# Two semaphore waits among GpSimd's indirect DMAs: every second scatter, and the third and fifth gather of a unit

## The chip, the cores and the metric

The kernel runs on one core of a Trainium2 chip. The metric is device time in microseconds (us) of one execution, taken without a profiler, as the median of several runs. Five engines work side by side on the core, each with its own stream of instructions in program order: PE (TensorE, matrix products), DVE (VectorE), ACT (ScalarE), POOL (GpSimd) and SP (SyncE, which here only issues DMAs). They meet through semaphores: an instruction or a DMA adds to a counter, and `wait_ge` holds an engine until a counter has reached a value. An engine that waits holds back all that stands behind in its stream. A DMA adds 16 to its semaphore in all, when all of it has landed.

## The reference, cut to what matters

There are 12,500 nodes with 64 features and 400,000 edges (`src`, `dst`, 16 attributes each), sorted by `dst`. A first graph network of three layers is followed by a second one that also uses the attributes, and each ends in a residual sum and a layer norm.

```
# first network, three times
agg = segment_sum((x * out_norm)[src], dst, 12500) * in_norm
x   = elu(agg @ W + b)
x   = layernorm(x0 + x)
# second network
ea  = edge_attr @ W_edge.T + b_edge
msg = relu(x[src] + ea)
h   = x + segment_sum(msg, dst, 12500)
h   = batchnorm(h @ W1.T + b1); h = relu(h); h = h @ W2.T + b2
out = layernorm(x + h)
```

What matters for the change is `x[src]` of the second network: for each edge, the row of the source node is needed.

## The kernel before, in words

**Counting (about the first 2,000 us of the profile).** A matrix of counts is built, how many edges lead from each node to each other node, window by window of 512 destination nodes, and stored in HBM (`counts`). With it the three layers of the first network become dense matrix products. POOL issues indirect DMAs here too (L997, L1006), which the change doesn't touch.

**Dense stage.** For 3 layers times 25 windows SP loads the counts back in pieces of 896 KB, seven to a window (L789, `load_piece`), and PE multiplies them (L2182). A piece is only loaded over an old one when PE has used that (semaphores `s_pused`). Beside it the edges of the first five windows of nodes are sorted by source block: 1,430 tiles of 128 edge records of 72 bytes, ten tiles to a "granule", 143 granules. SP loads a granule (`take_records`, L796) into one of two buffers, and before that waits until the granule two back has wholly been scattered (`s_put`). PE and DVE rank the records (L1428 to L1450). POOL then waits for the load (`s_take`) and for the ranks of five tiles (`s_rowi`), and writes each tile with one indirect DMA to its rows of `sorted_recs` in HBM (L1051, `put_records`): 1,430 scatters. SP's stream is in order and written out: piece loads and record loads stand in one row, a record load after about every 3.75 piece loads.

**Edge stage.** It begins when the scatters and the dense stage are done. There are 345 units of five tiles of unsorted edges. For each tile POOL gathers 128 rows of 256 bytes from `table32` in HBM into SBUF (L1086, `gather_units`): 1,725 gathers. Their buffers are a ring of six units; before a unit POOL waits until DVE has used the unit six back (`s_gmsg`). DVE adds the gathered rows to the edge terms (`add_rows`, L1652), ACT and PE follow. Beside the units the sorted records are handled in 294 "chunks", nearly one for every unit: DVE L1645, L1673, L1680, PE L2304 to L2344. DVE's order within a step with a chunk is: prepare the next chunk, chunk hots (L1673), source hot (L1645), `add_rows` (L1652), chunk low (L1680), unit hots (L1660), unit low (L1665).

**Tail.** About 100 us: the end of the batch norm, the last product, the layer norm and the stores.

On POOL nothing but the change's own two places is edited. All of the work after the counting stage that POOL does is the two lines L1051 and L1086, and both issue indirect DMAs whose descriptors POOL itself writes. The semaphores that the change waits on exist already: `s_put` (two, by the granule's parity) is waited for by SP (L795, L886) and DVE, `s_grow` (six, by the unit's place in the ring) by DVE (L1648).

Of the kernel before, what the change touches and what calls it, by code (L numbers as in the profile page):

```python
# [28 lines left out]
UNIT = 5  # L29
GRAN = 2 * UNIT  # L30
# [274 lines left out]
STEP_OF = [n * GATHERS // len(CHUNKS_S) for n in range(len(CHUNKS_S))]  # L305
CHUNK_IN = {step: j for j, step in enumerate(STEP_OF)}
UNIT_NODES = 224


def node_range(g):  # L310
# [7 lines left out]
def plan_bases():  # L318
# [4 lines left out]
    while sum(r[1] for r in runs) < len(ranges):  # L323
        at = sum(r[1] for r in runs)
        best = None
        for base in range(max(SORTED * WIN, ranges[at][1] - UNIT_NODES), ranges[at][0] + 1):
            for step in range(2 * GRAN * P // 16):
                n = 0
                while at + n < len(ranges) and ranges[at + n][1] - UNIT_NODES <= base + n * step <= ranges[at + n][0]:
                    n += 1  # L330
# [8 lines left out]
UNIT_BASE = [BASES[n // 2] for n in range(GATHERS)]  # L339
UNIT_WINDOWS = [sorted({b // WIN, (b + UNIT_NODES - 1) // WIN}) for b in UNIT_BASE]  # L340
BEGINS = {w: min(n for n in range(GATHERS) if w in UNIT_WINDOWS[n]) for w in range(SORTED, WINDOWS)}
# [6 lines left out]
ROW_RING, REC_RING, ATTR_RING, HOT_RING = 6, 4, 4, 4  # L348


def gnn_kernel(nc, x, src, dst, dst_rows, edge_runs, edge_recs, attr, w_l0, b_l0, w_edge, b_edge, w1, b1, gamma, beta,
               w2, b2, out):
    ctx = ExitStack()
    with ctx:
# [148 lines left out]
        def keys_of(a, b):  # L503
            return keys_a[:, a:b] if b <= KEYS_A else keys_b[:, a - KEYS_A:b - KEYS_A]
# [38 lines left out]
        c_hot = tmp16[:, 0:2 * CHUNK_TILES * WIN].rearrange("p (s k n) -> p s k n", s=2, k=CHUNK_TILES)  # L543
        g_hot = onehot_h[:, 0:HOT_RING * UNIT * UNIT_NODES].rearrange("p (s k n) -> p s k n", s=HOT_RING, k=UNIT)
        g_base = tmp_row[:, CHUNK_TILES * WIN:CHUNK_TILES * WIN + len(BASES)]
# [142 lines left out]
        s_put, PUT0 = s_near[2:4], [16 * (b - a) for a, b in SETS[2:4]]  # L688
# [7 lines left out]
        s_grow = [*gathered_sems.rows[0], *gathered_sems.rows[1], *gathered_sems.rows[2]]  # L696
# [245 lines left out]
        def _(pool):  # L942
# [100 lines left out]
            def put_records():  # L1043

                for g in range(RANKED // GRAN):
                    pool.wait_ge(s_take[g % 2], TAKE0[g % 2] + 16 * (g // 2 + 1))
                    for n in range(2):
                        pool.wait_ge(s_rowi, ROWI0 + g * 2 + n + 1)
                        for k in range(UNIT):
                            t = (g * 2 + n) * UNIT + k  # L1050
                            G.indirect_dma_start(out=sorted_recs[:, :], out_offset=bass.IndirectOffsetOnAxis(ap=keys_of(t, t + 1).bitcast(I32), axis=0),  # L1051
                                                 in_=taken[g % 2][:, n * UNIT + k, :], in_offset=None).then_inc(s_put[g % 2], 16)

            rank_tables()
            put_records()
            pool.wait_ge(s_bounds, 1)
            pool.wait_ge(s_bounds, 1)
# [21 lines left out]
            def gather_units():  # L1079

                for n in range(GATHERS):
                    if n >= ROW_RING:
                        pool.wait_ge(s_gmsg, n - ROW_RING + 1)
                    for k in range(UNIT):
                        t = (FIRST_UNIT + n) * UNIT + k
                        G.indirect_dma_start(out=g_rows[:, n % ROW_RING, k, :], out_offset=None, in_=table32[:, :],  # L1086
                                             in_offset=bass.IndirectOffsetOnAxis(ap=src_key[:, t:t + 1], axis=0)).then_inc(s_grow[n % ROW_RING], 16)

# [8 lines left out]
            with pool.Else():  # L1097
                pool.wait_ge(s_dtable, 16 * WINDOWS)
                bases(g_base).then_inc(s_bases, 1)
                gather_units()  # L1100

        @block.vector
        def _(dve):
# [4 lines left out]
            def link(ins):  # L1108

                chain[1] += 1  # L1110
                ins.then_inc(chain[0], 1)
                dve.wait_ge(chain[0], chain[1])
# [121 lines left out]
            def edge_bounds():  # L1234
# [14 lines left out]
                over, under = (g_ext[0:1, 2 + n, 0:len(BASES)] for n in range(2))  # L1249
                link(V.scalar_tensor_tensor(out=over, in0=greatest, scalar=-float(UNIT_NODES), in1=base_check, op0=ALU.add, op1=ALU.is_ge))  # L1250
                link(V.scalar_tensor_tensor(out=under, in0=least, scalar=float(SORTED * WIN), in1=base_check, op0=ALU.max, op1=ALU.is_lt))
# [373 lines left out]
            def sorted_edge_sums():  # L1625
# [29 lines left out]
                def unit_hots(n):  # L1655
                    if n >= HOT_RING:
                        dve.wait_ge(s_gused, n - HOT_RING + 1)
                    for k in range(UNIT):
                        t = (FIRST_UNIT + n) * UNIT + k
                        last = V.tensor_scalar(g_hot[:, n % HOT_RING, k, :], iota_win[:, 0:UNIT_NODES], dst_key[:, t:t + 1], None, ALU.is_equal)  # L1660
                    last.then_inc(s_ghot, 1)
# [791 lines left out]
```

## Time and profile before

| | us |
|---|---|
| median of 3 runs | 5930.82 (5928.49 to 5935.44) |
| span of the profiled execution | 7586.7 |
| POOL busy | 3774.9 (50% of the span) |
| PE busy | 5556.9 (73%) |
| DVE busy | 4274.3 (56%) |
| ACT busy | 2271.1 (30%) |

The profiled execution's own time is given by its span alone; it is 1,656 us, or 28%, longer than the median of the unprofiled runs. So the profile says how long instructions and landings take and in which order things happen, but it has gaps that the unprofiled runs can't all have. "Busy" for POOL is the time in which it writes the descriptors of an indirect DMA; the transfer itself comes later and is seen only as packets of the DMA queue q0 (software_dynamic). Queue q1 holds what SP issues. In the rows, "remote" and "another core or an unknown queue" are waits whose releaser the profile can't name, on a single core, and "issue" is time in which the engine waited for nothing that is shown.

### The profile page before, as it was taken

Reading aid. Unit: us, or ns where it says so; the run is one execution under the profiler, and the core shown is the slowest. Engines: PE = TensorE matmul, PEld = TensorE weight load, DVE = VectorE, ACT = ScalarE, POOL = GpSimd, SP = SyncE. Lnnn points to the kernel's source line nnn. Section 1 sums busy time; section 2 is a strip of 40 time slices with the busy share of each in tenths; the row PEclk is TensorE's granted clock in tenths of the full one; section 3 lists DMA queues with packets and bytes.
Section 4 is the critical chain, followed back from the end, with each engine's and each line's share of the span. In section 5 each row is a group of like instructions: output and inputs, shape, how many; then the busy total and the mean of one; then the engine's idle time right before and its main releaser. Section 6 shows DMA issues by size and latency. Waiting matters only on the chain.

```text
span 7586.7 us, 112214 instructions
## 1 busy us (share of the span) xinstructions
PE 5556.9 (73%) x39907; PEld 3224.8 (43%) x39908; DVE 4274.3 (56%) x14548; ACT 2271.1 (30%) x4057; POOL 3774.9 (50%) x3824
## 2 busy tenths in 40 slices
PE   6599799997777777778777774666766666665666
PEld 5366566665433333333433332333433333333334
DVE  5488888899533333333444112666666665555556
ACT  2487688873100000000001111333333322222223
POOL 4323233354354544545554556565655666665663
PEclk9799899999888988888888886888888888878887
DMA  2333333331555655556556661111111111111111
GB/s 99 140 130 119 120 142 137 118 118 64 177 173 188 197 177 180 186 186 195 184 185 193 218 207 41 32 34 33 33 33 33 34 33 32 33 33 32 32 32 34
DMA packets 438341, 828.25 MB, mean 109 GB/s; under 512 B 161611, under 2 KB 266983, under 8 KB 430951
## 3 DMA queue, kind: packets, MB, share of 16 engines
q1 hardware_dynamic: 305430, 713.88, 27.9%
q0 software_dynamic: 117952, 81.54, 5.1%
q10 hardware_dynamic: 14400, 25.61, 1.2%
q8 instruction: 323, 5.29, 0.3%
q14 instruction: 236, 1.93, 0.1%
HBM read 621.34 MB, written 199.35 MB: 108 GB/s over the span
## 4 chain that ended last, share of the span: by engine, by line
PE 24%; another core or an unknown queue 14%; issue 13%; DVE 11%; PEld 2%; ACT 1%; PEldq 0%; DVEq 0%; ACTq 0%
PE banks L2182 10%; PE banks L2344 4%; DVE tmp L1673 4%; PE banks L2271 2%; PE banks L2304 2%; PEld banks L2182 2%; DVE onehot L1660 2%; DVE rows_f L1652 2%; PE banks L2324 2%; PE banks L2331 1%; PE banks L2164 1%; DVE rows_f L1680 1%; DVE rows_f L1665 1%; PE banks L2157 1%
## 5 line engine op out<-in xcount | busy, mean ns | idle before, releaser
L1086 POOL DMA_INDIRECT rows_f<-table,src_key x1725 | 1708.4, 990 | 1103.4 <-DVE rows_f L1652 604.3
L1051 POOL DMA_INDIRECT sorted_recs<-onehot,rows x1280 | 1235.5, 965 | 1260.6 <-DMA onehot<-edge_recs_dram 718.7
L2182 PE MATMUL banks<-wide,rows_f 128*128 128x512 fp8e4 (+1 forms) x4900 | 1268.1, 400 | 355.4 <-issue 352.3
L1867 ACT ACTIVATE wide<-banks 128x784 fp8e4<-128x784 f32 x1563 | 1205.6, 825 | 484.6 <-PE banks L2104 340.6
L1006 POOL DMA_INDIRECT onehot<-edge_runs_dram,rows_f x472 | 596.2, 1263 | 1149.1 <-DVE onehot L1196 935.9
L2104 PE MATMUL banks<-rows_f 128*128 128x196 f16 (+2 forms) x7525 | 1004.1, 258 | 223.6 <-ACT wide L1867 138.7
L2104 PEld LDWEIGHTS banks<-rows_f 128*128 128x128 f16 x7525 | 708.5, 152 | 612.1 <-ACT wide L1867 401.9
L2271 PE MATMUL banks<-w_edge_blk,rows 80*128 80x320 f32 x690 | 337.4, 578 | 762.9 <-DVE rows_f L1652 521.6
L1444 DVE SCALAR_TENSOR_TENSOR onehot<-banks,onehot 128x98 f16<-128x98 f32 (+2 forms) x1113 | 295.6, 266 | 989.9 <-PE banks L2164 504.1
L1342 DVE TENSOR_TENSOR rows_f<-hid 128x1024 f16<-128x1024 f16 (+1 forms) x1016 | 679.4, 669 | 300.8 <-PE banks L2104 169.5
L1645 DVE TENSOR_SCALAR rows_f<-banks,iota_p 128x512 f16<-128x512 f32 x294 | 220.7, 751 | 1067.0 <-remote 638.8
L2182 PEld LDWEIGHTS banks<-wide,rows_f 128*128 128x128 f16 x4900 | 454.9, 103 | 817.2 <-issue 510.3
L2069 PE MATMUL banks<-wide,onehot 128*128 128x392 fp8e4 x3125 | 791.5, 334 | 9.2 <-issue 8.9
L2182 PE MATMUL banks<-wide,hid 128*128 128x512 fp8e4 (+1 forms) x2450 | 650.1, 401 | 126.3 <-issue 125.2
L1347 DVE TENSOR_TENSOR rows_f<-rows_f,tmp 128x1568 f16<-128x1568 f16 (+1 forms) x874 | 714.4, 817 | 0.0
L2344 PE MATMUL banks<-tmp,rows_f 128*128 128x512 f16 x2058 | 676.6, 485 | 0.0
L1673 DVE TENSOR_SCALAR tmp<-iota_win,rows 128x512 f16<-128x512 f16 x2058 | 638.0, 379 | 0.0
L1899 ACT ACTIVATE rows_f<-banks 128x512 f16<-128x512 f32 (+1 forms) x294 | 160.0, 544 | 1146.8 <-remote 671.6
L2271 PEld LDWEIGHTS banks<-w_edge_blk,rows 80*128 80x128 f32 x690 | 126.0, 228 | 825.3 <-issue 824.7
L2157 PE MATMUL banks<-onehot 128*128 128x98 f16 (+2 forms) x1113 | 244.1, 219 | 160.2 <-DVE onehot L1444 101.1
L2344 PEld LDWEIGHTS banks<-tmp,rows_f 128*128 128x128 f16 x2058 | 233.5, 120 | 295.3 <-issue 198.3
L1660 DVE TENSOR_SCALAR onehot<-iota_win,dst_key 128x224 f16<-128x224 f16 x1725 | 353.6, 287 | 0.0
(345 smaller groups left out, 7312.1 us busy)
## 6 DMA issues: line engine op xcount, KB each, us to landing
wide<-counts SPq DMA_DIRECT2D x504, 896.0 KB
counts<-wide SPq DMA_DIRECT2D x50, 3136.0 KB
rows_f<-table,src_key POOLq DMA_INDIRECT x1725
sorted_recs<-onehot,rows POOLq DMA_INDIRECT x1280
sorted_recs<-rows SPq DMA_DIRECT2D x28, 640.0 KB
rows<-attr_dram SPq DMA_DIRECT2D x345, 40.0 KB
onehot<-edge_recs_dram SPq DMA_DIRECT2D x143, 90.0 KB
agg_a<-attr_dram ACTq DMA_DIRECT2D x50, 250.0 KB
```

The lines of the kernel that those rows point to most:

```text
L1006: G.indirect_dma_start(out=stage[:, c % STAGES, j, :], out_offset=None, in_=edge_runs[:, :], in_offset=bass.IndirectOffsetOnAxis(ap=run_id ...
L1051: G.indirect_dma_start(out=sorted_recs[:, :], out_offset=bass.IndirectOffsetOnAxis(ap=keys_of(t, t + 1).bitcast(I32), axis=0), in_=taken[g ...
L1086: G.indirect_dma_start(out=g_rows[:, n % ROW_RING, k, :], out_offset=None, in_=table32[:, :], in_offset=bass.IndirectOffsetOnAxis(ap=src_k ...
L1342: V.tensor_tensor(lo_ring[:, s, :, 0:size], iota_lots[:, :, 0:size], lo_cols[:, n:lot.end].rearrange("p (o n) -> p o n", o=1).to_broadcast ...
L1347: V.tensor_tensor(key_ring[:, s, 0:size * cells].rearrange("p (n j e) -> p n j e", n=size, e=2), iota_key[:, 0:cells].rearrange("p (o j e) ...
L1673: last = V.tensor_scalar(c_hot[:, s, k, :], iota_win[:, :], c_dst[:, s, k:k + 1], None, ALU.is_equal)
L1867: A.activation(win_counts[o.half % 2][:, :, d0:d0 + o.quads * QUAD].rearrange("p b (q c) -> p b q c", c=QUAD), counted, ACT.Copy, scale=UN ...
L2069: M(out_ps.rearrange("p (b d) -> p b d", d=QUAD), ident16[:, :], win_counts[o.half % 2][:, :, d0:d0 + QUAD], start=False, stop=False)
L2104: last = M(octet_ps[n % 2][:, q, at:at + item.width * BLOCKS], lo, key, start=fresh[q], stop=True, skip_group_check=True)
L2182: last = M(acc_d[m % 2].rearrange("p (h d) -> p h d", h=2)[:, 0:h, :], layer_rows[n][:, block, :], pieces[:, PLACE[k], 0:h, c * HALF:(c + ...
L2271: M(g_ps, g_attr[:, n % ATTR_RING, :], w_edge_blk[0:UNIT * EDIM, 0:UNIT, :].rearrange("p k f -> p (k f)"), start=True, stop=True).then_inc ...
L2344: last = M(c_acc, c_two[:, s, k, :], c_hot[:, s, k, :], start=False, stop=False)
```

## The change

POOL gets waits on its own DMAs' semaphores. Ahead of scatter t with t even (and not 0) it waits until scatter t-1, and all before it on that semaphore, have landed. In a unit of gathers, numbered k = 0 to 4, it waits ahead of k = 2 until gathers 0 and 1 of the unit have landed, and ahead of k = 4 until gathers 0 to 3 have. No instruction is moved to another place, and no other engine is changed.

```diff
+LANDED_BEFORE = (2, 4)
...
                         for k in range(UNIT):
                             t = (g * 2 + n) * UNIT + k
+                            if t and t % 2 == 0:
+                                last, at = (t - 1) // GRAN, (t - 1) % GRAN
+                                pool.wait_ge(s_put[last % 2], PUT0[last % 2] + 16 * (GRAN * (last // 2) + at + 1))
                             G.indirect_dma_start(out=sorted_recs[:, :], ...
...
                     for k in range(UNIT):
                         t = (FIRST_UNIT + n) * UNIT + k
+                        if k in LANDED_BEFORE:
+                            pool.wait_ge(s_grow[n % ROW_RING], 16 * (UNIT * (n // ROW_RING) + k))
                         G.indirect_dma_start(out=g_rows[:, n % ROW_RING, k, :], out_offset=None, in_=table32[:, :],
```

## Rows read from the trace of the kernel before

**Rows 1.** The page, its chain of waits: share of the span by engine.
```profile
PE 24%; another core or an unknown queue 14%; issue 13%; DVE 11%; PEld 2%; ACT 1%; PEldq 0%; DVEq 0%; ACTq 0%
```
**Rows 2.** Busy time by stretch: counting, dense (two), edges, tail; us, then engines.
```profile
0.00:1990.00 1990.00, 1666.16 (x16203) 1149.23 (x16205) 1570.91 (x2981) 1297.33 (x1938) 685.38 (x663) 0.94 0.33 122
1990.00:4420.00 2430.00, 1838.72 (x10079) 876.17 (x10078) 900.33 (x5409) 117.42 (x190) 1236.92 (x1282) 0.87 0.59 188
4420.00:4670.00 250.00, 143.52 (x619) 63.63 (x617) 38.22 (x109) 23.57 (x32) 143.43 (x149) 0.74 0.42 134
4670.00:7490.00 2820.00, 1844.97 (x12639) 1081.72 (x12639) 1693.71 (x5912) 799.75 (x1840) 1709.14 (x1731) 0.82 0.14 33
7490.00:7587.00 97.00, 63.55 (x370) 54.07 (x370) 71.12 (x141) 33.02 (x59) 0.00 (x0) 0.63 0.15 34
```
**Rows 3.** The page, costliest groups: count, busy, mean ns, idle before and its releaser.
```profile
L1086 POOL DMA_INDIRECT rows_f<-table,src_key x1725 | 1708.4, 990 | 1103.4 <-DVE rows_f L1652 604.3
L1051 POOL DMA_INDIRECT sorted_recs<-onehot,rows x1280 | 1235.5, 965 | 1260.6 <-DMA onehot<-edge_recs_dram 718.7
```
**Rows 4.** What POOL waited for: us in total, times, longest.
```profile
POOL sorted_recs L1051 <- DMA onehot<-edge_recs_dram: 775.2, 90, 18.6
POOL rows_f L1086 <- issue: 498.9, 1513, 1.7
POOL sorted_recs L1051 <- issue: 407.4, 1323, 1.6
POOL sorted_recs L1051 <- DVE rows L1450: 171.5, 16, 79.9
```
**Rows 5.** Timeline of POOL, a unit of gathers: start, us, idle before.
```profile
5012.83 0.94 POOL L1086 DMA_INDIRECT rows_f<-table,src_key  x1 [2.43 <-DVE rows_f L1652]
5014.08 1.26 POOL L1086 DMA_INDIRECT rows_f<-table,src_key  x1 [0.30 <-issue]
5016.89 0.95 POOL L1086 DMA_INDIRECT rows_f<-table,src_key  x1 [0.30 <-issue]
5018.14 0.94 POOL L1086 DMA_INDIRECT rows_f<-table,src_key  x1 [0.30 <-issue]
```
**Rows 6.** Busy time by stretch around the gather of 5018.14; last: clock, DMA, GB/s.
```profile
5019.04:5019.70 0.66, 0.00 (x0) 0.00 (x0) 0.00 (x0) 0.15 (x1) 0.04 (x1) 1.00 0.00 0
5019.70:5020.20 0.50, 0.00 (x0) 0.00 (x0) 0.18 (x1) 0.14 (x1) 0.00 (x0) 1.00 0.25 66
5020.20:5021.40 1.20, 0.09 (x1) 0.12 (x2) 1.20 (x3) 0.32 (x2) 0.00 (x0) 1.00 0.00 0
```
**Rows 7.** DMA queues, 5019.70 to 5020.25: packets, MB, share.
```profile
q0 software_dynamic: 32, 0.03, 23.1%
```
**Rows 8.** Timeline of POOL, single scatters of three granules.
```profile
3340.21 0.96 POOL L1051 DMA_INDIRECT sorted_recs<-onehot,rows  x1 [6.95 <-DMA onehot<-edge_recs_dram]
3341.47 0.96 POOL L1051 DMA_INDIRECT sorted_recs<-onehot,rows  x1 [0.30 <-issue]
...
3364.92 0.96 POOL L1051 DMA_INDIRECT sorted_recs<-onehot,rows  x1 [0.30 <-issue]
3379.22 0.97 POOL L1051 DMA_INDIRECT sorted_recs<-onehot,rows  x1 [13.34 <-DMA onehot<-edge_recs_dram]
```
**Rows 9.** Busy time by stretch after the scatter of 3364.92.
```profile
3365.88:3366.38 0.50, 0.43 (x2) 0.00 (x0) 0.00 (x0) 0.00 (x0) 0.00 (x0) 0.50 0.00 0
3366.38:3366.70 0.32, 0.00 (x0) 0.00 (x0) 0.00 (x0) 0.00 (x0) 0.00 (x0) 0.50 0.22 29
3366.70:3368.50 1.80, 0.00 (x0) 0.00 (x0) 0.00 (x0) 0.00 (x0) 0.00 (x0) 0.50 0.00 0
```
**Rows 10.** DMA queues, 3341.17 to 3343.40, after the scatter of 3340.21.
```profile
q1 hardware_dynamic: 199, 0.66, 95.5%
```
**Rows 11.** DMA queues, 3343.40 to 3344.35.
```profile
q0 software_dynamic: 38, 0.01, 4.9%
```
**Rows 12.** Timeline of SP's queue, dense stage.
```profile
3348.40 0.47 SPq L796 DMA_DIRECT2D onehot<-edge_recs_dram  x1
3368.57 5.99 SPq L789 DMA_DIRECT2D wide<-counts  x3
```
**Rows 13.** Timeline of DVE, one step with a chunk.
```profile
5011.41 0.75 DVE L1645 TENSOR_SCALAR rows_f<-banks,iota_p 128x512 f16<-128x512 f32 x1 [2.87 <-PE banks L2304]
5012.08 0.48 DVE L1652 TENSOR_TENSOR rows_f<-banks,rows_f 128x320 f32<-128x320 f32 x1
5014.77 2.45 DVE L1673 TENSOR_SCALAR tmp<-iota_win,rows 128x512 f16<-128x512 f16 x8
5020.02 0.75 DVE L1645 TENSOR_SCALAR rows_f<-banks,iota_p 128x512 f16<-128x512 f32 x1 [2.80 <-remote]
```

## The prediction

> **What bounds the kernel now.** I read the chain of waits first. It names PE for 24% of the span, but also "another core or an unknown queue" for 14% (1,062 us) and "issue" for 13% (986 us) [rows 1]. On a single core an unnamed releaser for a seventh of the span is a warning: the profiled execution takes 7,587 us and the unprofiled runs 5,931, so 1,656 us of what the profile shows is not there when it counts, and these two entries, 2,048 us together, are where it can be. The reader should therefore not take the slack that POOL shows in the profile for slack.
>
> The busy time by stage comes next [rows 2]. The change touches the dense stage (1,990 to 4,670 us) and the edge stage (4,670 to 7,490). The counting stage (1,990) and the tail (97) have none of the new waits. If those two take unprofiled what they take here, 5,931 - 1,990 - 97 = about 3,840 us are left for the two touched stages, which take 5,500 under the profiler.
>
> Then POOL's own lines. A gather keeps POOL busy for 0.99 us in the mean and a scatter for 0.965 [rows 3]; between two of them 0.30 us pass with nothing waited for [rows 5, 8]. From start to start that is 5018.14 - 5016.89 = 1.25 us for a gather and 3341.47 - 3340.21 = 1.26 for a scatter. The 1,725 gathers and 1,430 scatters are 3,155 such steps, 3,155 x 1.25 = 3,944 us. That is more than the 3,840 us that the unprofiled run has for both stages. So unprofiled a step can't cost more than 3,840 / 3,155 = 1.22 us, and unless it costs far less, POOL is all but full from the first scatter to the last gather. The rest is close to it, but not over: DVE's step with a chunk is 5020.02 - 5011.41 = 8.61 us from one L1645 to the next, of which 2.80 is the unnamed wait [rows 13], so 5.81 without it, against POOL's 5 x 1.22 = 6.1 for a unit; PE is busy for 1,839 + 144 = 1,982 us in the dense stage, at a granted clock of 0.87 and 0.74 [rows 2], against POOL's 1,430 x 1.22 = 1,745.
>
> **What the change adds.** Nothing is taken away or moved. It adds 714 waits ahead of scatters and 2 x 345 = 690 ahead of gathers. What a wait costs POOL is the time from the end of an issue to its landing, plus the time to start once released, less the 0.30 us that passes anyway.
>
> *Gathers.* The issue of 5018.14 ends at 5019.08. No DMA engine works until 5019.70; then its 32 packets run, and after 5020.20 there is nothing [rows 6, 7]. So it lands about 1.15 us after the issue's end. For the start after a release I take the unit's first gather: DVE L1652 ends at 5012.56 and POOL starts at 5012.83 [rows 5, 13], 0.27 us. 1.15 + 0.27 - 0.30 = 1.1 us each. 690 x 1.1 = 759 us. Bounds: 0.85 if the release costs nothing (586 us), 1.5 if a landing is slower beside the attribute and record loads (1,035 us).
>
> *Scatters.* They are written to HBM beside the piece loads, which keep the DMA engines busy for 0.59 of the stage [rows 2]. Where nothing else runs, the scatter of 3364.92 (end 3365.88) has its packets between 3366.38 and 3366.70 [rows 9]: 0.8 us after the end, 0.8 + 0.27 - 0.30 = 0.77 us for the wait. Where pieces are loaded, the scatter of 3340.21 (end 3341.17) has no packet at all until 3343.40 [rows 10], and lands with the 32 or so that follow by 3344.35 [rows 11]: 3.2 us, or 3.15 for the wait. Many of the loads come in bursts with gaps between, so I go nearer to the quiet end: 1.4 us. 714 x 1.4 = 1,000 us; bounds 550 and 2,250.
>
> The Trainium skill ("DMA: Bandwidth & Descriptors", on the anatomy of a GpSimd DMA) gives about 2.0 us of fixed cost per DMA, most of it the receipt of the write, and says that the semaphore can be late above all for a write to HBM. The trace agrees for the gather (5018.14 to 5020.20, 2.06 us) but not for the quiet scatter, which goes to HBM and needs 3364.92 to 3366.70, 1.78 us; it is the company of other loads that makes it late. With 2.0 us for either, 1,404 waits would cost 2.0 - 0.95 + 0.27 - 0.30 = 1.02 us each, 1,430 us instead of my 1,759, an estimate by that page.
>
> *Who waits for POOL.* Behind a waiting scatter stand all later scatters. Their landing releases SP's load of the granule two on, and SP's stream is in order: behind that load stand the piece loads, and PE stands behind these: one record load and then three piece loads stand in that stream [rows 12]. So a slow POOL does not stay to itself: the dense stage becomes as long as the scatters. In turn POOL's present waits for the record load (775 us in 90 waits) and for the ranks (171 us) [rows 4] shrink, since SP can load the granule two on while POOL is still at the next. Behind a waiting gather stand the later gathers, and after at most six units DVE's L1652, which needs all five of its unit. The ring of six hides a late landing but no lower rate.
>
> *The sum.* For the unprofiled cost of a plain step I take 1.15 us, between the ceiling of 1.22 and 0.95, what is left if the 0.30 us were all the profiler's; nearer to the ceiling, because nothing says that POOL's gap is an artefact. POOL then needs 3,155 x 1.15 = 3,628 us, plus 759, plus 1,000: 5,387 us for the two stages, against 3,840. That is 1,547 more, with POOL without a pause. 5,931 + 1,547 = 7,478, and a few pauses for record loads remain at the start and between the stages, some 20 us: **7,500 us**.
>
> Against the profiled execution's own time: there a unit would go from its present 2,820 / 345 = 8.17 us to 5 x 1.25 + 2.2 = 8.45 or slightly more, and a granule from 2,665 / 143 = 18.6 to 10 x 1.26 + 5 x 1.4 = 19.6 or more (in the profile the dense stage also has its own gaps). So the profiled span should grow by far less than the median: by 100 us for the gathers and 150 to 500 for the scatters, to 7,850 to 8,300 us. The unprofiled runs have no such cushion, and the two should come near to each other.
>
> **The rivals.**
> *A. POOL is much faster without the profiler.* If a step costs 0.95 us or less, POOL has 3,840 - 2,997 = 843 us of pauses to fill first. With my waits that is 4,756 us, +916 us, 6,850. With both waits at their lower bound too, 2,997 + 586 + 550 = 4,133, +293, 6,220. For it: a fifth of the profiled span is gone in the unprofiled runs, and any engine may have its share. Against it: the busy part alone is 0.95 us and is the same from issue to issue.
> *B. The waits are hidden.* The profile itself would say so for the gathers: POOL has 8.17 - 6.25 = 1.9 us of pause in a unit, against 2.2 us of added waits. If the true unit were as long, only the scatters would cost: with a ring ahead of DVE, +50 us there and +100 to +300 in the dense stage, about 6,150. It needs the unprofiled time to be missing elsewhere, in the counting stage, where PE is busy for 1,666 of 1,990 us [rows 2]; I see no room for it. Wholly hidden, no change: only if a step cost below some 0.7 us.
> *C. Faster.* The waits thin out the queue of indirect DMAs. If scatters in flight hold up the piece loads, and gathers in flight hold up POOL's own descriptor writing (the second gather of a unit takes 1.26 us where others take 0.95 [rows 5]), then 345 x 0.3 = 103 us come back, and 5% on the dense stage's loads, some 80 us. It beats the waits only if these fall into pauses of POOL, so from the same point as B on: 5,931 - 183 = 5,750 us. Against it: q0 has 5% of the DMA time where q1 has 95% just before [rows 10, 11], and the slow second gather stands beside DVE's work and comes when the queue has just been empty.
> *D. Worse.* If the scatters' landings are at the busy end throughout (714 x 2.4 = 1,714 us) and the order of SP's stream makes POOL and PE wait in turn, the sum is 3,628 + 759 + 1,714 = 6,101, +2,261, 8,190.
>
> **How the numbers follow.** The forecast with POOL full and waits near 1.1 and 1.4 us has 0.68 (7,100 to 8,000). A has 0.14 (6,200 to 7,100), B 0.05, of which 0.02 for no measurable change, C 0.04, D 0.09. Two in ten may be left out: B, C, half of D and the lower part of A go, which gives 6,700 to 8,050. The least difference that a measurement of this kernel can tell is about 0.2%, 12 us. Faster by more than that: 0.04. Within it: 0.03. Slower: 0.93.
>
> **What would show it right or wrong.** In the profile after, POOL's timeline of a unit should read 0.30, 1.4, 0.30, 1.4 us of idle time ahead of gathers 1 to 4, the waits ahead of gathers should be released by a DMA or by an unnamed queue for 690 x 1.4 = 970 us, and POOL's wait on L1652 should nearly be gone. In the dense stage every second scatter should have 1 to 3.5 us ahead of it, POOL's waits on the record load should shrink from 775 us, and PE's L2182 should stand more, behind SP. Wrong would be: a median below 6,700 (the step or the slack is not what I think), pauses ahead of a waiting gather below 0.8 or above 2 us, POOL's wait on L1652 still above 300 us, or busy times of L1051 and L1086 that fall.

## The result, and the profile after

The changed kernel takes 8,462 us (8,461.81 to 8,469.93, 4 runs) and the kernel before 5,933 on the same chip: a ratio of 1.427, interval 1.4253 to 1.4288. That is 2,529 us more, where 1,567 were forecast, and it lies above the forecast range.

One thing has to be known to read the numbers. The runs fell on chips of two kinds. On one ("quick" here) the kernel before takes 5,926 to 5,939 us, on the other ("slow") 7,594 to 7,794, by the same instructions. Apart from that, one execution of `e6` took 8,749 us at a granted clock of 0.57, and the ratios leave it out. The medians of the prediction are from a quick chip, the profile it read is, by all signs, from a slow one: two later profiles of the kernel before from slow chips have the same stages and waits, and there the unprofiled runs are as long. The profile of the changed kernel is from a quick chip, and its span of 8,459.9 us is its time.

Its chain of waits has turned over. Before, it named PE and unnamed queues [rows 1]; now DMAs (46%, of which 44 are POOL's own transfers by the lines of the chain) and POOL (19%) hold 65% of it.
```profile
DMA 46%; POOL 19%; issue 13%; PE 12%; DVE 6%; ACT 4%; POOLq 0%; SPq 0%; DVEq 0%; ACTq 0%
```
Busy time by stretch of the changed kernel (counting, dense, edges, tail), answering to [rows 2]. The first number after the stretch is its length; PE, PEld, DVE, ACT and POOL follow, then PE's clock, the DMA share and GB/s.
```profile
0.00:1820.00 1820.00, 1643.77 (x16224) 1144.82 (x16226) 1574.22 (x2992) 1295.35 (x1938) 680.36 (x663) 0.97 0.37 133
1820.00:5172.00 3352.00, 2045.98 (x10676) 984.70 (x10673) 976.82 (x5515) 141.65 (x223) 1373.35 (x1430) 0.80 0.41 146
5172.00:8378.00 3206.00, 2038.92 (x12803) 1176.38 (x12803) 1719.52 (x5960) 814.51 (x1859) 1643.54 (x1732) 0.78 0.14 29
8378.00:8460.00 82.00, 48.40 (x206) 43.52 (x206) 54.69 (x82) 24.10 (x37) 0.00 (x0) 0.52 0.17 40
```
The counting stage ends at 1,820 us, not at 1,990. The two touched stages last 3,352 + 3,206 = 6,558 us. POOL is busy for no longer than before in either (1,373 and 1,644): all that is added is pause. What POOL waited for (us in total, times, longest), answering to [rows 4]:
```profile
POOL sorted_recs L1055 <- DMA sorted_recs<-onehot,rows: 1602.3, 639, 5.8
POOL rows_f L1092 <- DMA rows_f<-table,src_key: 1245.5, 690, 3.4
...
POOL rows_f L1092 <- issue: 316.7, 1035, 0.5
POOL sorted_recs L1055 <- issue: 219.1, 701, 2.2
POOL sorted_recs L1055 <- DMA sorted_recs<-onehot,hid: 152.4, 74, 5.2
```
The new waits stand there by name. 690 ahead of gathers took 1,245.5 us, 1.805 each; 713 ahead of scatters took 1,754.7, 2.46 each. Less the 0.305 us that pass anyway (316.7 in 1,035), they cost 1.50 and 2.16 us. The waits on L1652 and on the record load that POOL had before [rows 4] are gone from the list.

The timeline of POOL in a unit of gathers (start, us, idle before), answering to [rows 5]:
```profile
6511.13 0.94 POOL L1092 DMA_INDIRECT rows_f<-table,src_key  x1 [0.30 <-issue]
6513.82 0.94 POOL L1092 DMA_INDIRECT rows_f<-table,src_key  x1 [1.75 <-DMA rows_f<-table,src_key]
6515.07 0.94 POOL L1092 DMA_INDIRECT rows_f<-table,src_key  x1 [0.30 <-issue]
6518.83 0.94 POOL L1092 DMA_INDIRECT rows_f<-table,src_key  x1 [2.81 <-DMA rows_f<-table,src_key]
```
The issue of 6511.13 ends at 6512.07. Its packets all lie between 6512.75 and 6513.30, as this row of the DMA queues for that stretch shows, and from 6513.30 to 6513.82 no queue moved a packet:
```profile
q0 software_dynamic: 32, 0.03, 35.1%
```
Yet the next gather starts only at 6513.82, 0.5 us after the last packet. The chain of waits over the same stretch (start, us, what) splits this pause; a DMA's piece in it runs from the start of its issue until its semaphore is complete.
```profile
6511.13 2.44 DMA rows_f<-table,src_key
6513.56 0.26 issue
6513.82 0.94 POOL rows_f L1092
```
The semaphore is complete at 6513.56, which is about 0.3 us after the last packet and 1.5 us after the issue's end. From there POOL needs 0.26 us to start, and by the trace it does so in each of the 690 waits. So the prediction's 0.27 us for the start after a release was right. What it missed is that the landing comes later than the last packet: it put the landing 1.15 us after the issue's end.

The timeline of POOL in the dense stage shows both ends of a scatter's wait, 1.43 us where it is alone and 4.8 where it isn't:
```profile
3002.43 0.96 POOL L1055 DMA_INDIRECT sorted_recs<-onehot,rows  x1 [4.77 <-DMA sorted_recs<-onehot,rows]
3003.70 0.95 POOL L1055 DMA_INDIRECT sorted_recs<-onehot,rows  x1 [0.30 <-issue]
3006.08 0.96 POOL L1055 DMA_INDIRECT sorted_recs<-onehot,rows  x1 [1.43 <-DMA sorted_recs<-onehot,rows]
```
The chain splits the quiet one in the same way: the landing is 1.16 us after the issue's end (3004.65), though by the trace no packet runs after 3005.45, 0.8 us after it.
```profile
3003.70 2.12 DMA sorted_recs<-onehot,rows
3005.81 0.27 issue
```
The other engines wait for POOL, as the list of waits shows for DVE's sum of the gathered rows and for PE, which stands before pieces of counts that SP loads late:
```profile
PE banks L2188 <- DMA wide<-counts: 1171.5, 136, 16.0
...
DVE rows_f L1658 <- DMA rows_f<-table,src_key: 1116.1, 343, 8.5
```

### The profile page after: what moved, and what is told of

Its sections match the earlier page's. It is cut to its first block, busy times and chain, and to the rows that moved or that the text cites. A ratio compares the mean times of both kernels' runs of the same rounds, so it can differ in the third digit from the quotient of the medians.

```text
span 8459.9 us, 112214 instructions
## 1 busy us (share of the span) xinstructions
PE 5777.1 (68%) x39907; PEld 3349.4 (40%) x39908; DVE 4325.2 (51%) x14548; ACT 2275.6 (27%) x4057; POOL 3697.2 (44%) x3824
## 4 chain that ended last, share of the span: by engine, by line
DMA 46%; POOL 19%; issue 13%; PE 12%; DVE 6%; ACT 4%; POOLq 0%; SPq 0%; DVEq 0%; ACTq 0%
DMA sorted_recs<-onehot,rows 22%; DMA rows_f<-table,src_key 20%; POOL rows_f L1092 12%; POOL sorted_recs L1055 8%; PE banks L2110 4%; PE banks L2075 3%; ACT wide L1873 3%; DMA sorted_recs<-onehot,hid 2%; DVE rows_f L1353 2%; DVE rows_f L1348 2%; PE banks L2082 1%; PE banks L2188 1%; DMA wide<-counts 1%; PE banks L2020 1%; DMA agg_a<-attr_dram 0%
## 5 line engine op out<-in xcount | busy, mean ns | idle before, releaser
L1092 POOL DMA_INDIRECT rows_f<-table,src_key x1725 | 1642.6, 952 | 1562.3 <-DMA rows_f<-table,src_key 1245.5
L2188 PE MATMUL banks<-wide,rows_f 128*128 128x512 fp8e4 (+1 forms) x4900 | 1330.9, 421 | 795.6 <-DMA wide<-counts 786.6
L2277 PE MATMUL banks<-w_edge_blk,rows 80*128 80x320 f32 x690 | 382.6, 648 | 1286.6 <-DVE rows_f L1658 1162.5
L2188 PEld LDWEIGHTS banks<-wide,rows_f 128*128 128x128 f16 x4900 | 472.9, 107 | 1279.7 <-DMA wide<-counts 675.0
L2188 PE MATMUL banks<-wide,hid 128*128 128x512 fp8e4 (+1 forms) x2450 | 676.9, 415 | 389.9 <-DMA wide<-counts 385.0
L2350 PE MATMUL banks<-tmp,rows_f 128*128 128x512 f16 x2058 | 750.6, 527 | 0.0
L1658 DVE TENSOR_TENSOR rows_f<-banks,rows_f 128x320 f32<-128x320 f32 x345 | 169.6, 492 | 1116.3 <-DMA rows_f<-table,src_key 1116.1
L1940 ACT ACTIVATE rows_f<-rows_f 128x320 f16<-128x320 f32 x345 | 162.1, 470 | 1308.0 <-DVE rows_f L1658 1308.0
L2188 PEld LDWEIGHTS banks<-wide,hid 128*128 128x128 f16 x2450 | 226.2, 106 | 577.7 <-DMA wide<-counts 343.7
L2350 PEld LDWEIGHTS banks<-tmp,rows_f 128*128 128x128 f16 x2058 | 252.2, 129 | 338.2 <-issue 271.5
```

What stands on the lines that cost most here:

```text
L2188: last = M(acc_d[m % 2].rearrange("p (h d) -> p h d", h=2)[:, 0:h, :], layer_rows[n][:, block, :], pieces[:, PLACE[k], 0:h, c * HALF:(c + ...
L2277: M(g_ps, g_attr[:, n % ATTR_RING, :], w_edge_blk[0:UNIT * EDIM, 0:UNIT, :].rearrange("p k f -> p (k f)"), start=True, stop=True).then_inc ...
L2350: last = M(c_acc, c_two[:, s, k, :], c_hot[:, s, k, :], start=False, stop=False)
```

## The experiments

The theory after the result: on a quick chip POOL was full in both stages of the kernel before, a plain step takes 1.25 us, and a wait costs what is left of the landing, plus the release, less 0.30 us. The rivals are named with each run. `e1` to `e4` and `e13` to `e15` ran on quick chips, `e5` to `e12` on slow chips; each is compared with the kernel before on its own chip.

**The scatter waits alone** (`e1`). The two added lines among the gathers are taken out again:
```diff
-                        if k in LANDED_BEFORE:
-                            pool.wait_ge(s_grow[n % ROW_RING], 16 * (UNIT * (n // ROW_RING) + k))
```


> Only the waits ahead of every second scatter. Theory T (POOL is full without the profiler, a plain step costs 1.25 us, and a wait costs its landing and release less 0.30 us: in the changed kernel's profile 1,755 us in 713 waits, 2.46 us each, so 2.16 us of cost): 714 x 2.16 = 1,542 us, 5,933 + 1,542 = 7,475 us. Rival S (POOL has slack before, and the cost comes from SP's stream, in which the piece loads stand behind the record loads, so the waits of both kinds add up otherwise): not within 100 us of 7,475, and the changed kernel's 8,462 isn't the sum of the two halves. The profile's own span should lie near the time in the dense stage, if it was POOL's dense row of issues that the profiler drew out.

Measured: 7,436 us against 5,931, ratio 1.2537 (1.2516 to 1.2557), +1,505 us. The theory said 7,475. So by the time a scatter's wait costs 1,505 / 714 = 2.11 us, against 2.16 by the list of waits; where the other 37 us of the list went is not shown.

**The gather waits alone** (`e2`). The three added lines among the scatters are taken out:
```diff
-                            if t and t % 2 == 0:
-                                last, at = (t - 1) // GRAN, (t - 1) % GRAN
-                                pool.wait_ge(s_put[last % 2], PUT0[last % 2] + 16 * (GRAN * (last // 2) + at + 1))
```


> Only the waits ahead of the third and fifth gather of a unit. Theory T: in the changed kernel's profile 1,245 us in 690 waits, 1.805 us each, so 1.505 us of cost each and 1,038 us in all: 5,933 + 1,038 = 6,971 us. Rival S (slack of POOL in the edge stage before, some 1.9 us in a unit as in the profile of before): 690 x 1.505 less 345 x 1.9 = 655, so +380 us, 6,315.

Measured: 6,961 us, ratio 1.1736 (1.1716 to 1.1755), +1,030 us; theory 6,971, rival S 6,315. The two halves add up to 1,505 + 1,030 = 2,535 us, and both together cost 2,529. So no share that can be measured comes from their working on each other, and there is no slack that the first wait would have used up. POOL's list of waits in this run has the gathers' at the same size as in the changed kernel:
```profile
POOL rows_f L1089 <- DMA rows_f<-table,src_key: 1251.2, 690, 3.6
```

**As many waits, for what has long landed** (`e3`), as lines added to the kernel before:
```diff
+                            if g >= 2 and t % 2 == 0:
+                                pool.wait_ge(s_put[g % 2], PUT0[g % 2] + 16 * GRAN * (g // 2))
...
+                        if k in LANDED_BEFORE and n:
+                            pool.wait_ge(s_grow[(n - 1) % ROW_RING], 16 * UNIT * ((n - 1) // ROW_RING + 1))
```


> The same number of waits at nearly the same places, but for DMAs that have landed long before: ahead of every second scatter for the granule two back in full, ahead of the third and fifth gather for the unit before in full. Theory T (it is the landing that costs, not the instruction that waits): 5,933 us, within 20. Rival W (a wait on POOL costs by itself, because the next issue can't be prepared behind it): at 0.3 us each for 1,400 waits +420 us, 6,350.

Measured: 5,934 us, ratio 1.0005 (0.9996 to 1.0015). Some 1,400 waits cost nothing that can be measured, so rival W falls: it is the landing that is paid. POOL's list of waits shows how little is left of them:
```profile
POOL rows_f L1091 <- issue: 520.0, 1707, 0.3
...
POOL rows_f L1091 <- DMA rows_f<-table,src_key: 8.9, 18, 0.9
```

**Four gathers of five** (`e4`): `range(UNIT - 1)` in POOL's loop, and DVE waits for 16 x 4 instead of 16 x 5.

> No waits; of each unit's five gathers the last is left out (its rows are what lies in the buffer), so that POOL issues 345 fewer. Theory T (POOL is full before): the edge stage falls from 345 x 6.25 = 2,156 us to the larger of POOL's 345 x 5.0 = 1,725 and DVE's 294 x 5.81 + 51 x 2.3 = 1,825, so 5,933 - 331 = 5,600 us (5,500 to 5,620). Rival S (slack of POOL in the edge stage): 5,933, nothing gained.

Measured: 5,519 us, ratio 0.9306 (0.929 to 0.9321), 412 us less. The kernel leaves out one gather in five, so its output is not the reference's; only its time is read. Rival S falls: POOL did set the pace of the edge stage before. The gain is larger than the 331 us expected, near the whole 345 x 1.25 = 431. The bound I had set by DVE's step of 5.81 us was too high; DVE looks like the next bound, busy for 1,680 of 1,770 us in this row of the run's busy times, but POOL waited for it for only 14.6 us in 25 waits, so POOL still sets the pace here too:
```profile
3660.00:5430.00 1770.00, 1482.04 (x12706) 942.14 (x12749) 1679.70 (x5940) 804.94 (x1854) 1342.87 (x1385) 0.98 0.22 46
```

**The kernel before once more** (`e5`, `e12`, `e13`), for its profile; nothing is edited.

> The kernel before, once more with a profile. The first profile of it had a span of 7,587 us, its unprofiled runs 5,931. Theory D (that one profile was disturbed, chance and not the kernel): the span is now 5,935 us within 30, the counting stage ends near 1,820 us, POOL's plain step is 1.25 to 1.27 us, and its waits on L1652 and on the record load are below 50 us. Rival P (the profiler always draws this kernel out): 7,400 to 7,700 again.

> The kernel before, for its profile. On a quick chip: span 5,935 us within 30, counting stage 1,820 us, POOL's plain step 1.25 to 1.27 us, POOL's waits on L1652 and on the record load below 50 us in all. On a slow chip: 7,600 us as before.

> The kernel before, for its profile; the only two profiles of it so far, and the one that the prediction read, are from slow chips (7,587 to 7,760 us), the median to predict from a quick one (5,931). On a quick chip, theory T (POOL is full): span 5,935 us within 30, counting stage 1,820 us, plain step 1.25 to 1.27 us, POOL's waits on L1652 and on the record load below 50 us in all. On a slow chip: 7,600 to 7,760 again.

Measured: 7,603, 7,760 and 5,928 us. Theory D (one disturbed profile) and rival P (the profiler) both fall, for the unprofiled runs beside `e5` and `e12` are as long (7,630 and 7,757 us), and on a quick chip the profiled execution is as short as the unprofiled ones. The time goes with the chip. The third run is the profile that the prediction lacked. Its busy times by stretch:
```profile
0.00:1820.00 1820.00, 1642.41 (x16231) 1144.19 (x16233) 1575.20 (x2995) 1295.08 (x1938) 694.04 (x664) 0.98 0.37 133
1820.00:3668.00 1848.00, 1744.54 (x10669) 901.55 (x10668) 977.75 (x5512) 141.59 (x223) 1382.28 (x1436) 0.98 0.81 265
3668.00:5852.00 2184.00, 1690.19 (x12811) 1030.72 (x12811) 1703.01 (x5968) 813.88 (x1863) 1652.61 (x1727) 0.89 0.21 42
```
and what POOL waited for in it:
```profile
POOL rows_f L1086 <- issue: 525.6, 1725, 0.3
POOL sorted_recs L1051 <- issue: 443.4, 1389, 2.9
...
POOL sorted_recs L1051 <- DVE rows L1450: 88.2, 31, 79.1
```
All 1,725 gathers follow one another after 0.305 us with nothing else between. (1,653 + 526) = 2,179 us of the edge stage's 2,184 are POOL's plain steps, 1.26 us each. In the dense stage 1,382 + 443 = 1,825 of 1,848 are. POOL was full, and each added pause goes into the end. The profile also has what the first one lacked, POOL in the chain of waits:
```profile
PE 38%; POOL 34%; issue 14%; DVE 8%; ACT 5%; DMA 1%; POOLq 0%; DVEq 0%; ACTq 0%; SPq 0%
```
In the edge stage POOL and the 0.30 us between its issues are all of this chain. In the dense stage they are not alone: PE is busy for 1,745 of 1,848 us there, and the chain names its L2182 for 64% of that stage and POOL for 19%. Two engines were nearly full side by side, and `e1` shows that POOL had next to no slack beside PE.

**One wait, one step late** (`e6`, `e10`, `e14`): both waits of the change are out; in their place
```diff
+                        if k == 1 and n:
+                            pool.wait_ge(s_grow[(n - 1) % ROW_RING], 16 * UNIT * ((n - 1) // ROW_RING + 1))
```


> Gathers only: one wait in a unit, ahead of its second gather (k = 1), for the unit before in full. The last gather of that unit then ended 0.30 + 0.95 + 0.30 = 1.55 us before, and the pause ahead of a waiting gather in the changed kernel was 1.80 us in the mean. Theory T (only what is left of landing and release is paid): 345 x 0.25 = 86 us, 6,017 us (5,990 to 6,040). Rival R (the release costs 0.3 to 0.6 us of its own whenever a DMA of POOL's has to be waited for at all, whatever time has passed): 345 x 0.5 on top, 6,190.

> As e6: one wait in a unit, ahead of its second gather, for the unit before in full. On a quick chip, where POOL is full, Theory T: what is left of landing and release, 0.25 us each, 86 us, 6,017 us (5,990 to 6,040); rival R (0.5 us more for each wait that has to be waited for): 6,190. On a slow chip it is hidden in POOL's slack: no change, 7,630.

> One wait in a unit, ahead of its second gather, for the unit before in full. On a quick chip, theory T (only what is left of landing and release, 0.25 us, is paid): +86 us, 6,017 us (5,990 to 6,040); rival R (0.5 us more for each wait): 6,190. On a slow chip no change.

Measured: the first two on slow chips, ratios 0.9959 (0.9942 to 0.9976) and 0.9964 (0.9939 to 0.9989): hidden in POOL's slack there, and 0.4% faster if anything, which I can't explain. On a quick chip 6,035 us, ratio 1.0173 (1.0159 to 1.0186), +103 us; theory 6,017, rival R 6,190. POOL's list:
```profile
POOL rows_f L1089 <- issue: 420.8, 1381, 0.3
POOL rows_f L1089 <- DMA rows_f<-table,src_key: 201.2, 344, 2.1
```
201.2 / 344 = 0.585 us each, less 0.305 is 0.28, times 344 is 96 us. Of the 1.50 us that a wait costs right behind the gather, a wait one step (1.25 us) later costs 0.28.

**Every gather waits** (`e7`): no scatter waits, and `LANDED_BEFORE = (1, 2, 3, 4)`.

> Gathers only: a wait ahead of each of the second to fifth gather of a unit for all before it in the unit. Theory T: the cost is linear in the waits, 4 x 345 x 1.505 = 2,077 us, 8,008 us (7,950 to 8,060). Rival Q (part of a wait's cost is queueing behind the gather issued just before, and one alone lands sooner): a wait costs 1.1 instead of 1.5 us, 7,450.

Measured, on a slow chip: 9,095 us against 7,630, ratio 1.1926 (1.1888 to 1.1964). The expected time was for a quick chip. What can be compared is a wait's length, from POOL's list:
```profile
POOL rows_f L1089 <- DMA rows_f<-table,src_key: 2465.5, 1361, 3.0
```
1.81 us each, as with two waits in a unit of five (1.805 on the quick chip, 1,257.4 / 690 = 1.82 on a slow one in `e9`). Rival Q falls: a gather that is alone in flight lands no sooner.

**Scatter waits with small piece loads** (`e8`, `e11`, `e15`): as `e1`, and SP loads an eighth of each piece:
```diff
+                few = PB * HALF // 4 // 8
-                sp.dma_start(piece_words[:, PLACE[k], 0:h, :], counts[w, 0:h, :, k * PB * HALF // 4:(k + 1) * PB * HALF // 4]
+                sp.dma_start(piece_words[:, PLACE[k], 0:h, 0:few], counts[w, 0:h, :, k * PB * HALF // 4:k * PB * HALF // 4 + few]
```


> The scatter waits alone, as in the first experiment (7,436 us), but SP's piece loads bring in only an eighth of each piece of counts (seven eighths of the count matrix are left out; all instructions stay). Theory L (scatters land late because the piece loads are in the DMA engines' way): the waits fall from 2.46 us to the quiet 1.45, so 714 x 1.0 = 720 us less, 6,720 us. Rival H (they land late because HBM takes a scattered write slowly): 7,436, nothing gained.

> As e8: scatter waits alone, with an eighth of each piece of counts loaded (seven eighths of the count matrix are left out). On the slow chip the waits were 1,196 us in 705, 1.70 each. Theory L (piece loads hold up the scatters): 7,436 - 714 x (2.46 - 1.70) = 6,890 us on a quick chip, and 7,720 again on a slow one. Rival H (HBM takes a scattered write slowly): 7,436 on a quick chip.

> Scatter waits alone with an eighth of each piece of counts loaded (seven eighths of the count matrix are left out). On a quick chip, theory L (piece loads hold up the scatters): 7,436 - 714 x (2.46 - 1.70) = 6,890 us; rival H (HBM takes a scattered write slowly whatever else runs): 7,436. On a slow chip 7,720 to 7,810 again.

Measured: 7,717 and 7,811 us on slow chips (ratios 1.0127 and 1.0080 to the kernel before there), and 6,887 on a quick one, ratio 1.1618 (1.1600 to 1.1636), where theory L said 6,890 and rival H 7,436. POOL's list on the quick chip:
```profile
POOL sorted_recs L1056 <- DMA sorted_recs<-onehot,rows: 1070.0, 634, 4.3
...
POOL sorted_recs L1056 <- DMA sorted_recs<-onehot,hid: 121.8, 74, 2.9
```
1,191.8 / 708 = 1.68 us each instead of 2.46. The 6,890 is not a forecast from nothing: `e8` was expected to bring the wait down to 1.45 us and brought it to 1.70, and the later expectations use that 1.70. So 0.78 of the 2.16 us that a scatter's wait costs come from the piece loads in the DMA engines' way, and 7,436 - 6,887 = 549 us of the change's cost. Of what is left, 1.38 us, all but 0.25 is the cost of a quiet wait (1.43 - 0.30 = 1.13).

**The change on a slow chip** (`e9`), nothing edited.

> The changed kernel once more. The runs so far fell on chips of two kinds: the kernel before takes 5,931 us on one and 7,630 on the other, with PE held up for short times all through. Theory T (POOL full on the quick chip, slack on the slow one, a wait of the same length on both): on a quick chip 8,462 again. On a slow one the counting stage takes 1,980 us instead of 1,820, and POOL's 6,557 us for the other two stages stay, since POOL sets them: 8,462 + 160 = 8,620 us, a ratio of 1.13. Rival M (the ratio belongs to the kernel: 1.427 on either): 10,890 us on a slow chip.

Measured: 8,664 us against 7,757, ratio 1.1183 (1.1126 to 1.124). Theory T said 8,620, rival M 10,890. POOL's waits are as on the quick chip:
```profile
POOL sorted_recs L1055 <- DMA sorted_recs<-onehot,rows: 1587.9, 637, 6.0
POOL rows_f L1092 <- DMA rows_f<-table,src_key: 1257.4, 690, 3.4
```
With the waits POOL sets the pace on either chip, and the two differ by 2.4%; without them they differ by 31% (7,757 against 5,931; on the other slow chip, 7,630, by 29%).

## Why the prediction was wrong

The mechanism and the sign were right: POOL was full, each wait lengthens POOL's row, and nothing absorbs it (`e1`, `e2`, `e13`). The sizes of three terms were off, and they make up the miss of 962 us.

- **The scatter's wait, 1.4 us; it is 2.16.** 714 x 2.16 = 1,542 instead of 1,000, +542 us. Two steps failed. The quiet end was 0.77 us because I took the last packet, 0.8 us after the issue's end, for the landing; the landing is at 1.16, so a quiet wait costs 1.13 (+0.36). And I put the piece loads at 0.63 us above the quiet end, because they "come in bursts with gaps"; they add 1.03 (+0.40). `e15` shows the loads' share in it. It is not that they are denser than I read: the DMA share of the dense stage is 0.41 in the changed kernel, below the 0.59 of [rows 2], and the wait is as long on a slow chip (`e9`). How a scatter is held up among them no run here shows.
- **The gather's wait, 1.1 us; it is 1.50.** 690 x 1.50 = 1,038 instead of 759, +279 us. The last packet was placed nearly rightly, 1.15 us after the issue's end (1.2 in the unit shown above). The step that failed is "So it lands about 1.15 us after the issue's end": that is the last packet. The semaphore is complete 1.5 us after the issue's end in the unit shown, and 1.805 - 0.26 = 1.54 in the mean of the 690. The 0.27 us that I took for the start after a release, from a release by DVE, holds for a DMA too (0.26). The upper bound of 1.5 just met it, for another reason than the one given there.
- **The plain step, 1.15 us; it is 1.26.** I took a ceiling of 1.22 from 5,931 - 1,990 - 97 and then went below it. The 1,990 belonged to another chip; the counting stage takes 1,820 on the chip that the median came from. With 1,820 and a tail of 82 the same working gives a ceiling of (5,931 - 1,820 - 82) / 3,155 = 1.28. The profile's own 1.25 was right. Taken together, the plain steps and small pauses need 6,558 - 1,542 - 1,038 = 3,978 us instead of 3,648, +330, and the counting stage and the tail give back 170 + 15.

542 + 279 + 330 - 185 = 966 us, against 962 measured.

All three errors point the same way. None of the prediction's signs of being wrong showed: the waiting gathers' pauses lie between 0.8 and 2 us in the mean, POOL's wait on L1652 is gone, and the busy times of L1051 and L1086 are within 1% of those before on the same kind of chip. For the time the only such sign was a median below 6,700 us, none was set above, and 2 us as the upper limit of a gather's pause was too wide to catch 1.8. The forecast that could have told was the 970 us of waits ahead of gathers: they are 1,245.5.

Of the other steps: the claim that the profiler draws the execution out, on which "unprofiled" rests throughout, was false. The entry of 1,062 us for an unnamed queue belongs to the slow chips: the quick chip's chain hasn't got it. "Issue" is no artefact either, for it holds 14% there, 830 us (`e13`). The forecast for the profiled execution's own kind of chip, 7,850 to 8,300 us, was also low (`e9`: 8,664), and the same two waits were too short in it. That a slow POOL does not stay to itself was right: PE's L2188 waits for 1,172 us on pieces of counts in the changed kernel, where the same line before waited for 7 (`e13`). That the link is the order of SP's stream was read from the kernel, and no run tests it. Rivals A and B rested on slack that a quick chip hasn't; on a slow chip B is partly true: `e6` and `e10` cost nothing there, and the change costs 906 us (`e9`) instead of 2,529. Of C nothing was seen: POOL's busy times, 1,373 and 1,644 us in the two stages, are within 1% of those without waits (1,382 and 1,653, `e13`). D had the direction, and its scatter's wait of 2.4 us was nearer to the 2.16 than my 1.4. Its other half, POOL and PE waiting in turn through SP's stream, added nothing: POOL has no wait for a record load in the changed kernel, and the parts add up.

The Trainium skill's 2.0 us ("DMA: Bandwidth & Descriptors", anatomy of a GpSimd DMA) is short for the gather in this kernel: the profile now gives 2.4 us in the median from issue to landing, and 0.94 + 1.75 = 2.7 until the next issue starts. Its remark that the semaphore follows late on the write bears on what I left out, since I had measured to the last packet and called that the landing: from there to the complete semaphore it is about 0.3 us for the gather and 0.4 for the scatter shown above.

## What to carry to other kernels

A wait for an engine's own last DMA costs the whole landing and release, here 1.5 us for a gather and 2.2 for a scatter beside heavy loads, wherever that engine is full; for a gather, the same wait one step later costs 0.3 (`e14`), and two steps later nothing (`e3`). The end of a DMA's packets is not its landing: measure from the issue to the semaphore, or to the start of something that waits for it. Set signs of being wrong on both sides of a forecast, and close enough to catch a miss of its size. And when a profile's span isn't the time of the runs, find out whether it is the same chip before calling its gaps the profiler's.

## What the runs showed of the hardware

A DMA's landing comes after its last packet, by about 0.3 us for the gather (6513.25 to 6513.56) and 0.4 us for the scatter shown (3005.45 to 3005.81), and POOL starts 0.26 to 0.27 us after it (6513.56 to 6513.82, 3005.81 to 3006.08).

The kernel before took 5,926 to 5,939 us on at least two chips and 7,594 to 7,794 on two others, with every count of packets the same and an undisturbed step of POOL at 1.25 to 1.27 us on all. Busy times of DVE and ACT are within 1% (4,274 us on the slow chip and 4,308 on the quick one; 2,271 and 2,273), PE's is not (5,557 and 5,121). Each chip was seen in one stretch of time only, so that it is the chip, and not what else went on then, is the likely reading and isn't shown. On a slow chip PE is held up with nothing that it waits for in the profile. The first row is the kernel before on a slow chip (the profile that the prediction read), the second on a quick one (`e13`): PE's wait ahead of the dense products, us in total, times, longest.
```profile
PE banks L2182 <- issue: 477.5, 224, 21.2
```
```profile
PE banks L2182 <- issue: 18.6, 71, 0.4
```
The granted clock is lower too over the dense stage (0.87 and 0.74 [rows 2], against 0.98), but whether that is cause or consequence of the pauses no run here tells. This line's row is 459 us of the 1,656 between the two kinds. What holds PE up stays open.
